# Attention of layer one: 40 instead of 24 tile pairs of maxima during the projections, two units of chunk one first, early key rows loaded by GpSimd's queue

## The reference, cut to what matters

```python
q = (x @ wq.T).reshape(b, t, NUM_HEADS, 2, HEAD_DIM)
k = (x @ wk.T).reshape(b, t, NUM_HEADS, 2, HEAD_DIM)
v = (x @ wv.T).reshape(b, t, NUM_HEADS, 2 * HEAD_DIM)
attn1 = _attn(q1, k1, v)      # softmax(q1 k1 * scale) v
attn2 = _attn(q2, k2, v)
attn = attn1 - lambda_full * attn2
attn = attn * rms * subln_w * (1.0 - LAMBDA_INIT)
return attn.reshape(b, t, NUM_HEADS * 2 * HEAD_DIM) @ wo.T
```

## Time and profile before

| what | us |
|---|---|
| median of 3 runs | 2339.46 |
| lowest and highest run | 2334.36, 2339.69 |
| span of the profiled execution (its own time; what lies around the span is not recorded) | 2343.7 |
| first matmul of the projections | 19.69 |
| first score of head 0 | 182.18 |
| first score of head 1 | 212.22 |
| last transposed output of layer one, start | 948.36 |

### The profile page before, as it was taken

One profiled execution on the slowest core, in us unless ns is written; L12 is line 12 of the kernel. 1 busy time (PEld: TensorE's weight loads), 2 busy tenths in 40 slices (PEclk: granted clock), 3 DMA queues, 4 the chain that ended last, 5 costly groups with the idle time before them and its releaser, 6 DMA issues. The chain is left out here.

```text
span 2343.7 us, 42028 instructions
## 1 busy us (share of the span) xinstructions
PE 2244.7 (96%) x14576; PEld 1296.7 (55%) x14576; DVE 1588.8 (68%) x3629; ACT 1241.6 (53%) x2486; POOL 930.8 (40%) x767
## 2 busy tenths in 40 slices
PE   6898999999999999799999999978999999999989
PEld 5673333333333333578888888857644444444377
DVE  2246899999999995454444443462489898988567
ACT  3115787878787878342222212251266666767644
POOL 4005888888999999520000000001012121211152
PEclk9999999999999999899999999989799999999999
DMA  5654232223222100220000000004613221230011
GB/s 199 153 146 56 67 45 29 29 40 45 29 29 39 19 2 2 68 72 21 8 27 27 27 27 27 1 1 125 142 19 43 43 40 26 43 44 2 2 45 55
DMA packets 58905, 109.00 MB, mean 47 GB/s; under 512 B 11932, under 2 KB 23196, under 8 KB 58712
## 3 DMA queue, kind: packets, MB, share of 16 engines
q1 hardware_dynamic: 57864, 103.39, 21.4%
q0 software_dynamic: 848, 3.15, 0.4%
HBM read 73.75 MB, written 31.46 MB: 45 GB/s over the span
## 5 line engine op out<-in xcount | busy, mean ns | idle before, releaser
L834 DVE TENSOR_REDUCE l_maxima<-l_p_ring 128x1 f32<-128x512 f32 x1280 | 814.0, 685 | 94.4 <-PE l_p_ring L568 76.9
L770 ACT ACTIVATE l_w_hi_prob<-l_p_work 128x512 f32<-128x512 f32 (+3 forms) x1280 | 600.2, 535 | 217.6 <-PE l_p_work L590 212.0
L568 PE MATMUL l_p_ring<-xT_all 48*128 48x512 f32 (+3 forms) x1680 | 489.9, 419 | 0.0
L590 PE MATMUL l_p_work<-xT_all 50*128 50x512 f32 (+3 forms) x1680 | 471.2, 417 | 0.0
L568 PEld LDWEIGHTS l_p_ring<-xT_all 48*128 48x128 f32 x1680 | 243.2, 185 | 334.3 <-DVE l_maxima L834 205.5
L522 POOL TENSOR_TENSOR l_part<-l_w_hi_prob,l_w_hi_prob 128x1024 f32<-128x1024 f32 x128 | 304.2, 2378 | 191.3 <-ACT l_w_hi_prob L770 151.9
L536 POOL TENSOR_SCALAR_AFFINE_SELECT l_w_hi_prob<-l_w_hi_prob 128x256 f32<-128x256 f32 x256 | 105.7, 419 | 520.8 <-ACT l_w_hi_prob L770 520.8
L522 POOL TENSOR_TENSOR l_part<-x_prob,x_prob 128x1024 f32<-128x1024 f32 x128 | 301.9, 2380 | 19.7 <-ACT x_prob L770 19.4
L590 PEld LDWEIGHTS l_p_work<-xT_all 50*128 50x128 f32 x1680 | 234.8, 185 | 129.9 <-ACT l_w_hi_prob L770 85.5
L770 ACT ACTIVATE x_prob<-l_p_work 128x512 f32<-128x512 f32 x512 | 275.3, 601 | 49.9 <-PE l_p_work L590 49.8
L610 PE MATMUL l_p_work<-l_w_hi_prob,v_all 128*32 128x512 f32 (+3 forms) x1536 | 301.2, 497 | 0.3 <-ACT l_w_hi_sums L723 0.2
(11 more groups left out here) (169 smaller groups left out, 3697.9 us busy)
## 6 DMA issues: line engine op xcount, KB each, us to landing
xT_all<-q_parts SPq DMA_DIRECT2D x180, 128.0 KB
q_parts<-l_part SPq DMA_DIRECT2D x64, 256.0 KB
xT_all<-k_parts SPq DMA_DIRECT2D x90, 128.0 KB
k_parts<-l_part SPq DMA_DIRECT2D x40, 256.0 KB
xT_all<-k_parts SPq DMA_DIRECT2D x90, 64.0 KB
x<-in_x_T SPq DMA_DIRECT2D x4, 1024.0 KB, 11.1
ffn_w<-in_L_ffn_gate_w_T SPq DMA_DIRECT2D x8, 512.0 KB, 3.6
ffn_w<-in_L_ffn_up_w_T SPq DMA_DIRECT2D x8, 512.0 KB, 4.9
```

The lines of the kernel that those rows point to most:

```text
L568: filling = pe.matmul(p_ring[:, L.bank_at["maxima", n, u, sub] % L.ring, 0:keys], q[i][rows, n % 2, qt * P:(qt + 1) * P], k[i][rows, L.k_h ...
L590: pe.matmul(p_score[:, at % SCORE_BANKS, off:CH], k[i][rows, L.k_head(n), kt * P:(kt + 1) * P], q[i][rows, n % 2, qc * CH + off:(qc + 1) * ...
L770: act.activation(prob[step % L.prob_ring][:, sub, off:CH], p_score[:, at % SCORE_BANKS, off:CH], ACT.Exp, scale=HD ** -0.5).then_inc(exped, 1)
L834: dve.tensor_reduce(to, scores, AX.X, ALU.max).then_inc(freed, 1)
```

## The change

- The first 40 pairs instead of 24 (2.5 heads) are spread over the projections, from the 17th item on instead of the 22nd, and so the shifts of heads 0 and 1 are made there. In the list this gives every fourth place two pairs in a row. Heads 0 to 31 keep their pattern; maxima run 2.5 heads ahead, and the last 2.5 heads have none.
- The first two units of chunk one (units 8 and 9) come before the value tiles of chunk zero. SP issues the load of couple one behind the store of unit 9.
- In layer one the key rows and the rows of ones of the first three couples are issued by POOL's queue, ten DMAs a couple, after its splitting of x; SP issues their six q DMAs. A new semaphore `k_in` counts POOL's loads, and PE waits for both.
- SP sends shift 1 behind the store of unit 31, ahead of loads four and five. Later loads move by one shift.
- DVE sums the squares of a head behind the reciprocal of the next head's outputs (`invert`) instead of ahead of it.

Layer two keeps its order of items.

```diff
+        self.early_shifts = first_pairs // len(self.pairs)
+        self.ahead = self.early_shifts - 1
+        self.shift_after, self.shift_at_end = {}, []
+        for n in range(self.early_shifts):
+            later = [x[1] for x in self.items[self.items.index(("shift", n)):] if x[0] == "unit"]
+            if len(later) > 1:
+                self.shift_after[later[1]] = n
+            else:
+                self.shift_at_end.append(n)
...
+        if self.joint:
+            first_values = work[MT:MT + QPC]
+            work[MT:MT + QPC + 2] = work[MT + QPC:MT + QPC + 2] + first_values
...
-        start = MT + QPC + EARLY_UNITS - 1 + LOAD_SLOTS
+        start = MT + 2 + LOAD_SLOTS if self.joint else MT + QPC + EARLY_UNITS - 1 + LOAD_SLOTS
         for i, item in enumerate(work):
             out.append(item)
-            if shift_at == i:
-                out.append(("shift", 0))
+            if i in shift_at:
+                out.append(("shift", shift_at[i]))
             while i >= start and at * (len(work) - start) < self.first_pairs * (i + 1 - start):
                 out.append(("pair", *divmod(at, len(self.pairs))))
                 at += 1
-                if at == len(self.pairs):
-                    shift_at = i + 1
+                if at % len(self.pairs) == 0:
+                    shift_at[i + 1] = at // len(self.pairs) - 1
...
-           24, (6, 12, 26))
+           40, (6, 12, 26))
...
+        POOL_LOADS = 16 * (STACK_LOADS // 2 + 2 * KH)
...
+        def k_by_pool(p):
+
+            return L.joint and p < 3
...
+        def wait_for_slot(engine, p):
+
+            i = slot(p)
+            if p == 0:
+                wait_stored(engine, MT + 2)
+                engine.wait_ge(ready, 3)
+            elif p > PAIR_RING:
+                engine.wait_ge(scored, (p - PAIR_RING + 1) * 4 * S)
+            else:
+                wait_stored(engine, QC * MT)
+                engine.wait_ge(v_done, NT // B * ((i - 1) // 2 + 1))
...
+                wait_for_slot(sp, p)
                 for sub in range(2):
                     for at in range(len(Q_PART)):
...
+                        load_q(sp, p, sub, at)
+                        if not k_by_pool(p):
+                            load_k(sp, p, sub, at)
+                    if p <= PAIR_RING and not k_by_pool(p):
+                        load_ones(sp, p, sub)
...
-                    if L.shift_store == at[0]:
-                        shift_row(0)
-                    if at[0] == MT + EARLY_UNITS - 1:
+                    if at[0] in L.shift_after:
+                        shift_row(L.shift_after[at[0]])
+                    if at[0] == (MT + 1 if L.joint else MT + EARLY_UNITS - 1):
                         load(0)
...
-            for n in range(1, HEADS):
+            for n in range(L.early_shifts, HEADS):
                 shift_row(n)
-                if n >= 4 and n % 2 == 0 and n // 2 - 1 + PAIR_RING < PAIRS:
-                    load(n // 2 - 1 + PAIR_RING)
+                couple, odd = divmod(n - L.ahead, 2)
+                if couple >= 2 and not odd and couple - 1 + PAIR_RING < PAIRS:
+                    load(couple - 1 + PAIR_RING)
...
+            for p in range(3):
+                if k_by_pool(p):
+                    wait_for_slot(pool, p)
+                    if p:
+                        pool.wait_ge(k_in, POOL_LOADS * p)
+                    for sub in range(2):
+                        for at in range(len(K_PART)):
+                            load_k(pool, p, sub, at, k_in)
+                        load_ones(pool, p, sub, k_in)
...
                 if u == 0:
                     pe.wait_ge(q_in[i], pair_loaded(n // 2))
+                    if k_by_pool(n // 2):
+                        pe.wait_ge(k_in, POOL_LOADS * (n // 2 + 1))
...
                     copy_shift(*at)
-                    if L.joint and at[0] >= 3:
-                        average(at[0] - 3)
                 elif what == "turn" and L.joint:
                     if at[1]:
                         invert(at[0])
+                        if at[0]:
+                            average(at[0] - 1)
```

More of the change, by code:

```diff
@@ L115, in __init__ @@
         self.items = self.projections() + self.heads()
-        later = [x[1] for x in self.items[self.items.index(("shift", 0)):] if x[0] == "unit"]
-        self.shift_store = later[1] if len(later) > 1 else None
+        self.early_shifts = first_pairs // len(self.pairs)
[7 more added lines that the diff above has]
+                self.shift_at_end.append(n)
         self.filled_at, self.bank_at, self.freed_at = {}, {}, {}
@@ L169, in heads @@
         ahead = SUM_LAG * (QC if self.joint else 1)
-        done = {"score": [ahead] * 2, "maxima": [self.first_pairs] * 2, "sum": 0, "ones": 0, "shift": 1}
+        done = {"score": [ahead] * 2, "maxima": [self.first_pairs] * 2, "sum": 0, "ones": 0,
+                "shift": self.first_pairs // len(self.pairs)}
         out, turns = [("score", *divmod(i, S), sub) for i in range(ahead) for sub in range(2)], []
@@ L373, in selected, with wait_stored, load_q, load_k @@
             return n * sum(diagonal(i) for i in range(S)) + sum(diagonal(i) for i in range(s + 1))
+        def wait_for_slot(engine, p):
[8 more added lines that the diff above has]
+                engine.wait_ge(v_done, NT // B * ((i - 1) // 2 + 1))
+        def wait_stored(engine, units):
+            for r in range(PART_BUFFERS):
+                engine.wait_ge(stored[r], 16 * PARTS * len(range(r, units, PART_BUFFERS)))
+        def load_q(engine, p, sub, at):
+            i, first = slot(p), 4 * p + sub
+            rows = slice(HALF * sub + at * HD, HALF * sub + (at + 1) * HD)
+            kept = slice(Q_PART[at] * HD, (Q_PART[at] + 1) * HD)
+            engine.dma_start(q[i][rows, :, :].bitcast(F32), q_parts_d[first:first + 3:2, kept, :].rearrange("s r t -> r s t")
+                             ).then_inc(q_in[i], 16)
+        def load_k(engine, p, sub, at, landed=None):
+            i, first = slot(p), 4 * p + sub
+            rows = slice(HALF * sub + at * HD, HALF * sub + (at + 1) * HD)
+            kept = slice(K_PART[at] * HD, (K_PART[at] + 1) * HD)
+            heads = slice(first, first + 3, 2) if KH == 2 else slice(p, p + 1)
+            engine.dma_start(k[i][rows, :, :].bitcast(F32), k_parts_d[heads, kept, :].rearrange("s r t -> r s t")
+                             ).then_inc(landed or q_in[i], 16)
+        def load_ones(engine, p, sub, landed=None):
+            i = slot(p)
+            for h in range(KH):
+                engine.dma_start(k[i][HALF * sub + SROWS:HALF * sub + FROWS, h, :].bitcast(F32),
+                                 ones_rows[:, :].bitcast(F32)).then_inc(landed or q_in[i], 16)
         @block.sync
@@ L427, in store @@
                                  part[u % PART_BUFFERS][i][:, :].bitcast(F32)).then_inc(stored[u % PART_BUFFERS], 16)
-            def wait_stored(units):
-                for r in range(PART_BUFFERS):
-                    sp.wait_ge(stored[r], 16 * PARTS * len(range(r, units, PART_BUFFERS)))
             if first_load:
@@ L448, in _ @@
                     break
[L449 to L451 removed]
+            for n in L.shift_at_end:
+                shift_row(n)
+            wait_stored(sp, L.units)
             load(3)
             load(4)
[L454 removed]
+            for n in range(L.early_shifts, HEADS):
                 shift_row(n)
[L456 to L457 removed]
+                couple, odd = divmod(n - L.ahead, 2)
+                if couple >= 2 and not odd and couple - 1 + PAIR_RING < PAIRS:
+                    load(couple - 1 + PAIR_RING)
             sp.wait_ge(shift_in, 64 * HEADS)
@@ L920, in _ @@
                         average(at[0] - 1)
-            for n in range(HEADS - 3 if L.joint else HEADS - 1, HEADS):
-                average(n)
+            average(HEADS - 1)
 def tile_pipeline(engine, *stages, written_out=WRITTEN_OUT):
```

31 lines of the change are left out of this document (5 added, 26 removed).

## The result

The changed kernel took 2348.07 us (median of 20 runs, 2337.64 to 2350.72) against 2343.83 for the kernel before beside it (20 runs, 2331.39 to 2347.2): a ratio of 1.0019, interval [1.001, 1.0028], so some 4 us slower. (The 2339.46 of the kernel before stands for the first three of its 20 runs, so the forecast is compared by its difference.) The forecast was 6.4 us faster, with a range from 13.5 faster to 5.5 slower; the change came out near its slow end.

What follows compares the result with a forecast made beforehand. TensorE, busy throughout layer one's heads, sets the pace, so added projection work pays only in its pauses. Terms -13.7 + 18.7 + 0.5 - 10.0 - 1.9 = -6.4 us, from 2339.46 to 2333.1; range 2326 to 2345.

Steps and rivals of the forecast that it cites:

- I take it as in time: Projections: couple one's load over two queues lands before the first pair; bounds 2.8 us early to 7.7 late.
- Rival one: Projections: both queues share one pace, +5.8 us at couple one, +3.2 at couple two, 2342.1 in all; chance 0.24.
- the 190: Start of the heads: a first score later than 190 us would show the forecast wrong.
- Pairs moved in: +18.7 us: Projections: 40 pairs, eight of them double, cost 34.5 us in place of 15.7 for 24 pairs.
- stalls taken out: Projections: the time lost around the loads of couples one and two goes, -13.7 us.
- at nothing: Parts costed at zero: unit order, splitting of x, GpSimd's new waits, SP's store wait, sum of squares behind `invert`.
- the second shift: Projections: making a second shift there costs +0.5 us, between nothing and one pair (0.655).
- the heads: Heads of layer one: wait for shift 1 and its lower clock gone, -10.0 us; one more head without maxima, -1.9.
- Rival two: Projections behind value tile 7: stores starve behind longer loads, 9.7 us on top of rival one's 5.8, 2348.6; chance 0.10.
- Rival three: Projections: doubles cost little more than single pairs, -8.2 us on the sum, 2324.9; chance 0.11.

Runs made afterwards that it cites:

- e2_sp: Changed kernel with all loads given back to SP's queue; 2348.46 us, ratio 1.0008 to the kernel before.
- e1_rev: Changed kernel with GpSimd issuing its key rows upper half of the partitions first; 2348.49 us, ratio 1.0011 to the kernel before.
- e13: Changed kernel with its 40 pairs begun one item later and GpSimd loading only couples one and two; 2347.11 us, ratio 1.0024 to the kernel before.
- e12: As e13, but the second pair of each double set into the next item; 2337.25 us, ratio 0.9972 to the kernel before.
- e9: Changed kernel with its 40 pairs begun two items later, nothing else changed; 2353.01 us, ratio 1.0037 to the kernel before.
- e4_split: Changed kernel with each double's second pair put behind the eighth of the next item's twelve matmuls; 2342.18 us, ratio 0.9995 to the kernel before.
- e10_pairs: Changed kernel with the old order of units and all loads on SP, 40 pairs kept; 2369.04 us, ratio 1.01 to the kernel before.

## Why the prediction was wrong, step by step

**The step that failed first: "I take it as in time"**, of the load of couple one. With GpSimd's issues at half a microsecond each, sooner than the 0.78 of the earlier trace rows, the load was still 2.34 us late (69.93), inside the bounds of 2.8 early to 7.7 late. The two queues moved 140 GB/s where SP alone moved 116 (e2_sp): a fifth more, where the reason given, different partitions, had them add up. In e1_rev, where the queues start in different halves, the load was still late by 1.79 us. Cost with the clock, beyond a double's own price: 4.4 us. Rival one put this at +5.8 and was right about this half; its other half, 3.2 us at couple two, did not come. The first score, at 194.99, is past the 190 that the prediction named as a sign of being wrong.

The Trainium skill, "DMA: Bandwidth & Descriptors", section "Issuing engines are not separate DMA queues", says that DMAs started by different engines run on the same 16 DMA engines and interleave, and that only the time to initiate them is saved. The trace agrees: the first pair came at 69.93 for 71.73 in e2_sp, 1.8 us sooner, and the last issue of the load ended at 61.39 for 64.20, 2.8 us sooner.

**"Pairs moved in: +18.7 us"** was sized well pair by pair: 2.07 measured for 1.98 behind a unit, 1.31 for 1.19 behind a value tile, and the waits were the expected ones. It left out the clock: two of the 1.35 us pauses were followed by the lower clock, 3.1 us together. It also treated the doubles as a cost of their own. e13 against e12 shows that they also make TensorE wait for late stores, so that the gain of "stalls taken out" can't be had beside them: in e9 and e13 the stall that the start was moved away from came back at the next double.

**The work costed "at nothing"** did not name GpSimd's 30 new DMAs at the end of the layer: 2.0 us of TensorE.

4.4 + 3.1 + 2.0 = 9.5, against the 9.2 us to be explained; what is left are differences of under 1 us each, of both signs. The rest came as forecast: the second shift 0.37 for 0.5 (a step of 3.74 on the ruler with a pair and the shift), the heads -11.4 for -11.9 (7.49 and the clock for shift 1 gone, as expected; the last heads, without maxima, are 21.59 and 22.04 us apart where 21.61 stood in the earlier trace rows):

```profile
894.28 1.09 PE L710 MATMUL l_p_ring<-ident,l_w_hi_sums 128*128 128x128 f32 x8
915.87 1.09 PE L710 MATMUL l_p_ring<-ident,l_w_hi_sums 128*128 128x128 f32 x8
937.91 1.09 PE L710 MATMUL l_p_ring<-ident,l_w_hi_sums 128*128 128x128 f32 x8
```

Rival two, starving stores behind value tile 7, did not occur in the changed kernel: ScalarE had no wait for a store over 2 us between 60 and 130, as the forecast said. A stall of that kind is what e9 and e13 show, at the first double. Rival three's gain, 8.2 us for doubles that cost little, is about what e4_split got by taking them apart, 6.8 at the first exponential; and e12, with the load not waited for either, has layer two at 1581.43, 6.6 us ahead of the kernel before. Shown by runs: the doubles (e4_split, and e12 against e13) and GpSimd's DMAs at the end. The wait for the late couple stands in the trace; taking it away gains nothing while the doubles are there (e9, e13), and with them apart a start one item later, with couple three back on SP, brings the first exponential 3.2 us sooner (e12 against e4). Argued alone: that the 1.4 us by which the medians differ beyond the start of layer two lie in layer two's two kinds; the means of the 20 runs differ by 3.4. Open: why two of the four 1.35 us pauses were followed by the lower clock and two were not.

## What to carry to other kernels

Work that is moved into a stage "because TensorE pauses there" must not need more buffers at once than the stage has free: two pairs in a row on a ring of three turned late stores into stops of TensorE (5.14 us in e9, 2.79 in e13), and setting the second one eight matmuls later was worth some 10 us. Splitting a load over two queues moved it by 1 to 2 us here and no more, and where the first pair no longer waited for the load, ScalarE waited for a store behind it (6.15 us in e9). Compare profiles at a point behind the change and ahead of stages that vary by themselves: here the spans alone had the wrong sign.

## What was unexpected of the hardware

- The end of the layer grows with the DMAs that GpSimd issued in it, 0.08 us each, long after they had landed (5, 15, 25, 35 DMAs: GpSimd's drain 1.26, 2.07, 2.89, 3.71 us).
- A pause of TensorE of 1.35 us can be followed by 3.4 us at a granted clock of 0.50: two of four in the changed kernel, six of seven in e10_pairs. The 10.2 us at 0.50 in e4_split had no pause of over 0.5 us in the 30 us ahead, and the same place of the work has no such stretch in the changed kernel.
- Two queues moved 140 GB/s together where one alone moved 116 in the same stretch (e2_sp), with the DMA engines busy for 0.91 and 0.95 of it. Letting the queues start in different halves of the partitions brought the first pair 0.45 us sooner (69.48 for 69.93) and the kernel nothing that shows.
